# Four graph layers on one core: layer 1 aggregates before it projects, its logits are dot products on VectorE, small operations go to GpSimd

## The reference, cut to what matters

```python
h = relu(layernorm(x)); x = x + L0(h)      # x: 128 graphs, 128 nodes, 256 features
h = relu(layernorm(x)); x = x + L1(h)
h = relu(layernorm(x)); x = x + L2(h)
h = relu(layernorm(x)); x = x + L3(h)      # multi-head attention, 8 heads of 32

def L1(h):
    Wh = h @ W                                  # 256 x 256
    logits = leaky_relu((Wh @ a_src)[:, :, None] + (Wh @ a_dst)[:, None, :], 0.2)
    attn = softmax(where(adj == 0, -inf, logits), axis=-1)
    return nan_to_num(attn, nan=0.0) @ Wh
```

## Time and profile before

| | us |
|---|---|
| median of 3 runs | 1276.25 |
| lowest, highest | 1275.59, 1278.63 |
| the profiled execution, its own time | 1276.93 |
| its span in the profile | 1275.1 |

### The profile page before, as it was taken

How to read it: one execution, slowest core, us unless ns; L and a number is a source line. 1 busy time by engine, 2 the same in 40 slices (tenths; PEclk the granted TensorE clock), 3 DMA queues, 4 the chain that set the end, 5 groups by cost and what they waited for, 6 DMA issues and landing times. The chain is left out here.

```text
span 1275.1 us, 43341 instructions
## 1 busy us (share of the span) xinstructions
PE 1232.8 (97%) x12213; PEld 1134.8 (89%) x12213; DVE 1141.8 (90%) x5713; ACT 1058.2 (83%) x3911; POOL 944.5 (74%) x1338
## 2 busy tenths in 40 slices
PE   5799999999999999999999999999999999999997
PEld 4689999999999999999999998999999999999986
DVE  4689999989999999999999999999999999998874
ACT  2468898888888888888889888888889888888886
POOL 4568877877777877777787787777787777787663
PEclk9899999999999999999999999999999999999999
DMA  4011222222112122222112122222122122211001
GB/s 119 24 22 21 38 44 50 37 44 51 36 44 52 36 44 52 36 43 52 38 40 52 40 45 46 41 39 52 40 47 43 41 46 44 43 39 31 18 19 34
DMA packets 70586, 53.57 MB, mean 42 GB/s; under 512 B 20688, under 2 KB 70352, under 8 KB 70352
## 3 DMA queue, kind: packets, MB, share of 16 engines
q1 hardware_dynamic: 68144, 49.35, 19.2%
q10 hardware_dynamic: 2208, 1.45, 0.4%
HBM read 33.89 MB, written 16.89 MB: 40 GB/s over the span
## 5 line engine op out<-in xcount | busy, mean ns | idle before, releaser
L775 ACT ACTIVATE exps<-masked,nmax 128x128 f32<-128x128 f32 x1024 | 397.1, 394 | 0.0
L348 POOL TENSOR_TENSOR probs<-exps,rsum 128x512 f32<-128x512 f32 x256 | 266.7, 1042 | 162.6 <-DVE rsum L567 161.9
L319 POOL TENSOR_SCALAR y<-x,nm,rstd 128x256 f32<-128x256 f32 x512 | 282.8, 563 | 22.5 <-issue 21.0
L311 POOL TENSOR_TENSOR rstd<-veps,power 128x2 f32<-128x2 f32 x256 | 178.2, 696 | 114.4 <-DVE veps L472 109.3
L559 DVE CUSTOM_DVE_ANT_0 masked<-bank,mask 128x128 f32<-128x128 f32 x1024 | 232.0, 280 | 1.3 <-PE bank L986 0.8
L775 ACT ACTIVATION_READ_ACCUMULATOR exps<-masked,nmax 128x1 f32 x1024 | 198.4, 194 | 0.0
L876 PE MATMUL bank<-w_hi,ht_hi 128*128 128x512 f32 (+1 forms) x512 | 192.6, 376 | 4.5 <-DVE ht_lo L501 4.5
L456 DVE BATCH_NORM_STATS2 stats<-x 128x6 f32<-128x256 f32 x512 | 183.9, 411 | 0.2
L886 PE MATMUL bank<-ident,y 128*128 128x128 f32 x1024 | 159.0, 278 | 20.0 <-POOL y L319 19.3
L877 PE MATMUL bank<-w_lo,ht_hi 128*128 128x512 f32 (+1 forms) x512 | 175.4, 343 | 0.0
L878 PE MATMUL bank<-w_hi,ht_lo 128*128 128x512 f32 (+1 forms) x512 | 174.8, 341 | 0.0
(11 more groups left out here) (120 smaller groups left out, 3693.4 us busy)
## 6 DMA issues: line engine op xcount, KB each, us to landing
x<-in_x SPq DMA_DIRECT2D x64, 256.0 KB, 4.6
out<-x SPq DMA_DIRECT2D x64, 256.0 KB, 4.7
db<-rows SPq DMA_DIRECT2D x110, 128.0 KB, 4.1
rows<-dst SPq DMA_DIRECT2D x110, 1.0 KB, 3.0
probs<-in_w0t SPq DMA_DIRECT2D x1, 512.0 KB, 7.9
probs<-in_w1t ACTq DMA_DIRECT2D x1, 256.0 KB, 5.9
exps<-in_wot SPq DMA_DIRECT2D x1, 256.0 KB, 7.6
w_sb<-in_w ACTq DMA_DIRECT2D x1, 256.0 KB, 7.8
```

The source lines that it names most:

```text
L311: pool.tensor_tensor(rstd[i][:, b], veps[i][:, b], power[:], ALU.pow).then_inc(S[f"rstd{i}"], 1)
L319: last = pool.tensor_scalar(y[i][:, b, g], src[:, bx, g], nm[i][:, s, g:g + 1], rstd[i][:, s, g:g + 1], ALU.add, ALU.mult)
L348: pool.tensor_tensor(probs3[:, p % BUFFERS["probs3"], j], exps3[:, p % BUFFERS["exps3"], j], rsum3[:, s, j].unsqueeze(2).to_broadcast([P, ...
L775: last = act.activation(exps3[:, b, j, i], masked3[:, p % BUFFERS["masked3"], j, i], ACT.Exp, bias=nmax3[:, s, j, i:i + 1], scale=-1.0, ac ...
```

## The change

What it does, part by part:

- Layer 1 no longer transposes and projects `h` first. GpSimd forms `y1` = relu(x1 - mean) without the factor of the deviation (`centre1`). TensorE multiplies it with the transposed exponentials (`u_mm`, four fp32 matmuls of 128 columns), the result is split (`u_hi` on ScalarE, `u_lo` on VectorE) and then projected (`x2_mm`, the twelve fp32r matmuls). `h1t`, `h1t_hi`, `h1t_lo`, `wh0_mm`, `wh1_mm`, `wh0`, `wh1` and the old `x2_mm` go.
- The factor 1/deviation of a neighbour's row is put into the transposed exponentials: `at1` is two ScalarE copies of 128 columns with a scale per partition.
- The logits: VectorE takes four products with sum over 256 columns (`dots`), two with W a_dst, which stays in PSUM bank 7 (`w_dst`), and two with W a_src in SBUF (`w_src`). GpSimd multiplies them by the deviation's inverse into `ed1` (`dst1`, now for each pair), and SP writes `ed1` to DRAM itself.
- `veps` of all layers and the clearing of `rsum1` move from VectorE to GpSimd. `nm` goes: the mean is subtracted in `y` directly.
- All lags, the order of each engine's list and the banks are new; `y1` has three buffers.

```diff
@@ GpSimd
+            def shifted_variance(i, p):
+                b = p % SMALL
+                passed(pool, f"mv{i}", p)
+                passed(pool, f"rstd{i}", p, SMALL)
+                pool.tensor_scalar(veps[i][:, b], mv[i][:, b, :, 1], LN_EPS, None, ALU.add).then_inc(S[f"veps{i}"], 1)
+            def clear_empty_rows(p):
+                s = p % SMALL
+                passed(pool, "rsum1_any", p)
+                pool.tensor_tensor(rsum[1][:, s], rsum[1][:, s], has_any[:].to_broadcast([P, G]), ALU.mult).then_inc(S["rsum1"], 1)
+            def centre1(p):
+                b, s, bx = p % BUFFERS["y1"], p % SMALL, p % BUFFERS["x1"]
+                passed(pool, "mv1", p)
+                read_before(pool, "y1", p, "dots", "u_mm")
+                for g in range(G):
+                    last = pool.tensor_scalar(y[1][:, b, g], x1[:, bx, g], mv[1][:, s, g, 0:1], 0.0, ALU.subtract, ALU.max)
+                last.then_inc(S["y1"], 1)
+            def scale_dots(p):
+                b, s = p % BUFFERS["ed1"], p % SMALL
+                passed(pool, "dots", p)
+                passed(pool, "rstd1", p)
+                read_before(pool, "ed1", p, "z1")
+                pool.tensor_tensor(ed1[:, b], dots[:, s], rstd[1][:, s].unsqueeze(1).to_broadcast([P, 2, G]), ALU.mult).then_inc(S["dst1"], 1)
@@ VectorE
-                dve.tensor_scalar(veps[i][:, b], mv[i][:, b, :, 1], LN_EPS, None, ALU.add).then_inc(S[f"veps{i}"], 1)
-                dve.tensor_scalar(nm[i][:, b], mv[i][:, b, :, 0], -1.0, None, ALU.mult).then_inc(S[f"nm{i}"], 1)
+            def dot_products(p):
+                b, s = p % BUFFERS["y1"], p % SMALL
+                passed(dve, "y1", p)
+                dve.wait_ge(S["w1_split"], 1)
+                passed(dve, "dst1", p, SMALL)
+                passed(dve, "dots", p, 1)
+                for c, w in ((1, w_dst), (0, w_src[:])):
+                    for g in range(G):
+                        last = dve.tensor_tensor_reduce(weighted[:, c, g], w, y[1][:, b, g], scale=1.0, scalar=0.0, op0=ALU.mult, op1=ALU.add,
+                                                        accum_out=dots[:, s, c, g:g + 1])
+                last.then_inc(S["dots"], 1)
+            def low_u(p):
...
+                dve.tensor_tensor(ut_r[1][:, b].rearrange("p c g n -> p (c g n)"), bank_of("u")[:],
+                                  ut_r[0][:, b].rearrange("p c g n -> p (c g n)").bitcast(F32), ALU.subtract).then_inc(S["u_lo"], 1)
@@ ScalarE
-                act.activation(wh[:, b, g], bank_of(f"wh{g}")[:, 0:D + 2], ACT.Copy).then_inc(S[f"wh{g}"], 1)
+            def high_u(p):
...
+                act.activation(ut_r[0][:, b].rearrange("p c g n -> p (c g n)"), bank_of("u")[:], ACT.Copy).then_inc(S["u_hi"], 1)
+            def scale_exp_transposed1(p):
...
+                for g in range(G):
+                    last = act.activation(at[1][:, b, g], bank_of("at1")[:, g * P:(g + 1) * P], ACT.Copy, scale=rstd[1][:, s, g:g + 1])
@@ TensorE
+            def aggregate1(p):
+                b, ba = p % BUFFERS["y1"], p % BUFFERS["at1"]
+                passed(pe, "at1", p)
+                bank_free(pe, "u", p)
+                for c in range(DC):
+                    for g in range(G):
+                        last = pe.matmul(bank_of("u")[:, (c * G + g) * P:(c * G + g + 1) * P], y[1][:, b, g, c * P:(c + 1) * P], at[1][:, ba, g],
+                                         start=True, stop=True)
+            def project1(p):
+                b = p % BUFFERS["ut"]
+                passed(pe, "u_lo", p)
...
+                for g in range(G):
+                    for c in range(DC):
+                        last = split_matmul(bank_of("x2b")[:, g * D:(g + 1) * D], [u_[:, b, c, g] for u_ in ut_r], [w_[:, c, :] for w_ in w1_r],
+                                            c == 0, c == DC - 1)
```

More of the change, by code:

```diff
@@ L29 @@
 LAG = {
[11 rows of a table removed]
[11 rows of a table added]
 }
 BANKS = {
[L45 to L48, removed]
-    "v": (0, "v_mm", ('v',)),
[L50 to L75, removed]
+    "h0t": (5, "h0t", ('h0t_lo',)),
+    "pt1": (3, "pt1", ('p3t_1',)),
+    "qt": (4, "qt_mm", ('qt',)),
+    "x1b": (6, "s0", ('x1',)),
+    "kt": (0, "kt_mm", ('kt',)),
+    "d1": (3, "d1", ('z1',)),
+    "at2": (2, "e2t", ('at2',)),
+    "ot": (4, "ot_mm", ('ot_lo',)),
+    "sc0": (5, "scores", ('nmax3_0',)),
+    "sc1": (1, "scores", ('nmax3_1',)),
+    "sc2": (0, "scores", ('nmax3_2',)),
+    "sc3": (6, "scores", ('nmax3_3',)),
+    "h2t": (2, "h2t", ('ht2',)),
+    "x3b": (3, "x3_mm", ('x3',)),
+    "m0": (4, "m0", ('mj_lo0', 't0_0')),
+    "at1": (6, "e1t", ('at1',)),
+    "hh": (2, "hh_mm", ('hh',)),
+    "pt2": (3, "pt2", ('p3t_2',)),
+    "pt3": (5, "pt3", ('p3t_3',)),
+    "prep": (6, "products", ('w1_split',)),
+    "u": (6, "u_mm", ('u_lo',)),
+    "m1": (3, "m1", ('mj_lo1', 't0_1')),
+    "x4b": (2, "x4_mm", ('x4',)),
+    "v": (0, "v_mm", ('v',)),
+    "h3t": (4, "h3t", ('h3t_lo',)),
+    "x2b": (2, "x2_mm", ('x2',)),
+    "pt0": (6, "pt0", ('p3t_0',)),
+    "d2": (1, "d2", ('z2',)),
+    "prepa": (6, "adj_spread", ('adj_rows',)),
     "zz2": (7, "z2", ('nmax2',)),
@@ L110, in gnn_kernel @@
         warm = sb("warm", [P, G])
-        w1_sb = sb("w1_sb", [P, DC, D + 2])
+        w1_sb = sb("w1_sb", [P, DC, D])
         a1_sb = sb("a1_sb", [P, DC, 2])
@@ L272, in step @@
                     spread_row(2, t - LAG["row_in2"])
+                if due(t, "load") and t - LAG["load"] >= 2:
+                    load(t - LAG["load"])
             load(0)
@@ L357, in step @@
             def step(t):
+                if due(t, "rstd3"):
+                    inverse_deviation(3, t - LAG["rstd3"])
+                if due(t, "y3"):
+                    normalise(3, x3, t - LAG["y3"])
+                if due(t, "dst1"):
+                    scale_dots(t - LAG["dst1"])
+                if due(t, "veps0"):
+                    shifted_variance(0, t - LAG["veps0"])
+                if due(t, "rsum1"):
+                    clear_empty_rows(t - LAG["rsum1"])
+                if t == LAG["deg_b_made"]:
+                    prepare_deg_b()
@@ new lines, in step @@
+                if due(t, "veps2"):
+                    shifted_variance(2, t - LAG["veps2"])
+                if due(t, "rstd2"):
+                    inverse_deviation(2, t - LAG["rstd2"])
+                if due(t, "y2"):
+                    normalise(2, x2, t - LAG["y2"])
+                if due(t, "p3_2"):
+                    normalise_p3(2, t - LAG["p3_2"])
+                if due(t, "p3_0"):
+                    normalise_p3(0, t - LAG["p3_0"])
+                if due(t, "p3_3"):
+                    normalise_p3(3, t - LAG["p3_3"])
@@ L390, in step @@
[L390 to L401, removed]
+                if due(t, "veps3"):
+                    shifted_variance(3, t - LAG["veps3"])
@@ L585, in step @@
             def step(t):
+                if due(t, "stats0"):
+                    stats_of(0, x0, t - LAG["stats0"])
+                if due(t, "nmax3_3"):
+                    mask_scores(3, t - LAG["nmax3_3"])
+                if t == LAG["w1_split"]:
+                    split_w1()
+                if due(t, "x3"):
+                    sum_x3(t - LAG["x3"])
+                if due(t, "nmax3_0"):
+                    mask_scores(0, t - LAG["nmax3_0"])
+                if due(t, "stats3"):
+                    stats_of(3, x3, t - LAG["stats3"])
@@ new lines, in step @@
+                if due(t, "t0_0"):
+                    add_own(0, t - LAG["t0_0"])
+                if due(t, "rsum3_1"):
+                    inverse_sum3(1, t - LAG["rsum3_1"])
+                if due(t, "u_lo"):
+                    low_u(t - LAG["u_lo"])
+                if due(t, "x4"):
+                    sum_x4(t - LAG["x4"])
+                if due(t, "rsum1_any"):
+                    inverse_sum(1, "rsum1_any", "x2", t - LAG["rsum1_any"])
+                if due(t, "mj_lo1"):
+                    low_mj(1, t - LAG["mj_lo1"])
@@ L1073, in step @@
                     attend(2, hh, "hh", F1, t - LAG["x3_mm"])
-                if due(t, "wh1_mm"):
-                    project1(1, t - LAG["wh1_mm"])
+                if due(t, "m0"):
+                    project0(0, t - LAG["m0"])
+                if due(t, "e1t"):
+                    transpose_exp(1, t - LAG["e1t"])
                 if due(t, "hh_mm"):
                     project2(t - LAG["hh_mm"])
+                if due(t, "pt2"):
+                    transpose_p3(2, t - LAG["pt2"])
+                if due(t, "pt3"):
+                    transpose_p3(3, t - LAG["pt3"])
+                if t == LAG["products"]:
+                    multiply_weights()
+                if due(t, "u_mm"):
+                    aggregate1(t - LAG["u_mm"])
+                if due(t, "m1"):
+                    project0(1, t - LAG["m1"])
+                if due(t, "x4_mm"):
+                    project4(t - LAG["x4_mm"])
+                if due(t, "v_mm"):
```

(11 more changed lines are left out.)

367 lines of the change are left out of this document (146 added, 221 removed), and 22 rows, old and new, of the table LAG.

## The result

The changed kernel takes 1453.3 us (median of 4, 1452.7 to 1454.4), the kernel before beside it 1276.6: a ratio of 1.138 (95% interval 1.136 to 1.140). I had said 1256, with 1243 to 1286 around it and 71% for faster. The profiled execution of after has a span of 1451.6 us.

What follows compares the result with a forecast made beforehand. TensorE was taken to bound the kernel, busy for the whole 18.88 us step. 1276.93 - 25.6 (TensorE) + 7.0 (64 steps of 18.59 against 18.48) - 2 (ends) = 1256.3 us, given as 1256, range 1243 to 1286.

Steps and rivals of the forecast that it cites:

- L: Hold of VectorE's two `w_src` products behind GpSimd: between 0 and 1.13 us a step, taken as 0.4.
- TensorE, -0.40 us a step: Transposes `h1t` (-0.44) and old `x2_mm` (-0.86) go, `u_mm` (+0.90) comes: 18.48 us a step.
- VectorE: Small operations removed, 1.53 us, `dots` added, 1.38 us: 17.85 to 17.70 us a step, plus L.
- rival (c): Both `w_src` products held for a whole `y3` operation: step 19.3 us, 1304 us; chance 0.18 with milder forms above 1280.
- my sign for L = 0: In the profile after, the two `w_src` products would show a mean of 0.42 us.
- GpSimd: Four `veps`, `rsum1` and `dst1` as a product add 1.0 us a step on 14.9, bounds +0.9 and +3.4.
- the ring: Once-a-step loop from GpSimd's `rsum1` over `x3_tail` to VectorE's `stats3` and back: 18.2 us + L.
- the small operations at the price of the power: Sign of being wrong: GpSimd's small operations cost like the power, lengthening the ring by 0.5 for each in it.
- a bad place in a list: Sign of being wrong: an order placed by hand makes TensorE wait in each step for something else.

Runs made afterwards that it cites:

- e9: e8 with `y1` one place later in ScalarE's list, behind `p3t_2` instead of in front of it; 1249.1 us, 0.979 of the kernel before.
- e1: The changed kernel with ADD in place of SUBTRACT in the two GpSimd lines that form `y` (values differ); 1286.9 us, 1.007 of the kernel before.
- e3: The changed kernel with `nm` computed again on VectorE right behind `mv`, and all `y` by ADD; 1350.3 us, 1.057 of the kernel before.
- e7: The changed kernel with `nm` made on GpSimd, `y` by ADD and `veps1` moved in front of `y1`; 1365.4 us, 1.068 of the kernel before.
- e8: e7 with `y1` formed on ScalarE by Relu with bias `nm1`, in front of `p3t_2`; 1268.5 us, 0.991 of the kernel before.
- e5: e1 with SUBTRACT in `y2` alone; 1368.5 us.
- e6: e1 with SUBTRACT in `y3` alone; 1310.9 us.
- e4: GpSimd alone, sixteen of each of fourteen forms in a row, nothing of the four layers computed; ADD,MULT 557 ns, SUBTRACT,MULT 1223.

## Why the prediction was wrong

It was GpSimd's `y`, whose operation the change exchanged and whose price the sum left as it was. Term by term, with the row of the changed kernel on which L is read in front:

```profile
L537 DVE CUSTOM_DVE_ANT_0 weighted<-w_src,y 128x256 f32<-128x256 f32 x128 | 49.9, 427 | 0.0
```

- **TensorE, -0.40 us a step: right.** e9's step is 18.43 with PE busy throughout, against 18.88: -0.45.
- **VectorE: right in direction, and L was small.** `dots` cost the 1.38 us of the sum (e1: 614.68 to 616.06), and VectorE is busy 19 us less over the run, 0.3 a step, where the sum had 0.15 less, plus L. L, the hold of the two `w_src` products, was the unknown on which I put the range and the losing rival (c). The changed kernel has a mean of 427 ns for them, against 418 for the products with PSUM, though GpSimd's `y3` runs beside both (2.44 us from 613.50; the products start at 613.97 and 614.31). That was my sign for L = 0. It is not 0 in each order: in e3 and e7 the mean is 511 and 507, because one of the two is 0.2 us longer in every step. Rival (c) as priced did not happen. By the Trainium skill (SBUF - State Buffer, section Who interferes with whom), as I read it, the later one waits for the whole of the other. The traces do not show that here: a product loses nothing in a step of the changed kernel and 0.2 us in one of e3 or e7, and GpSimd's `y3` can be the one that is longer, 1.57 us for 1.10 in e1 and 1.52 in e7.
- **GpSimd: the step that failed.** I wrote that GpSimd "gets four `veps` and `rsum1`, and `dst1` becomes a product", +1.0 us. I left `y` at 563 ns in the sum of the ring and nowhere costed that its operation had changed. The edit is in the diff and looked like a renaming: it takes away `nm`, and the price of that was 5.1 us on GpSimd against 0.4 saved on VectorE (4 x 0.07 + 0.11). The 1.0 us that I did add was right: `veps`, `rsum1` and the product, less the old copy, come to 73 us, 1.1 a step. The row I needed was not in the trace of before: no tensor_scalar of that size with any other pair had run there. So it should have been bounded, by a row of another form. The nearest, a two-input operation of 128x256 at 686 ns, gives 0.12 us more each and would still have been too low.
- **The ring: right in form.** It was written as 18.2 us + L, with 12.5 on GpSimd; e1 has 13.63 there, and 12.5 without the 2 x 0.58 of a slow `y1`. With `y0` and `y2` at 1.23 and `y1` at 1.14 in place of 0.56 each it is 18.2 + 4 x 0.66 + 2 x 0.58 = 22.0; measured 21.73. With `y1` alone slow it is 19.4; e1 has 19.09. The forecast by that ring and the right price would have been 1276.9 + 64 x (22.0 - 18.88) = 1477 us.
- **Sum.** Of the 197 us between 1256 and 1453, 166 are SUBTRACT's (e1 against after). The other 31 lie between the forecast and e1, and e9, with `y1` off GpSimd, stands 38 under e1. By the ring that part is `y1`'s ADD,MAX, 2 x 0.58 us a step. This is argued and not shown: no run had `y1` on GpSimd at the fast pair's price, and e8 and e9 bring `nm` back and move `veps1` too.
- **The chances.** Only L was given a range up to a loss. None of the signs of being wrong that I named was this one: they were the small operations at the price of the power, and a bad place in a list. A range has to cover each operation whose form the trace of before does not show, not only the one that a rule calls dangerous.

## What to carry to other kernels

An operation is a form: engine, instruction, size, and also the pair of ALU operations. When an edit changes the pair, its price is unknown until a row shows it, and on GpSimd it moved by a factor of 2.2. Add up each ring that passes once a step through in-order queues: work in the ring costs nearly one for one (e5: 82 us for 87), work outside it less than half (e6: 24 for 62), whatever the busy shares say. And an operation moved to a less busy engine still takes its place in a queue: one place later was worth 16 to 19 us here (e8, e9).

## What the runs showed of the hardware that I had not expected

- GpSimd tensor_scalar, 128x256 fp32 (e4): ADD,MULT and MULT,ADD 557 ns; SUBTRACT,MULT and MULT,SUBTRACT 1223; ADD or SUBTRACT with MAX 1143; one operation alone, ADD or SUBTRACT, 925, more than the fast pair takes for two. Per column 0.83 and 3.3 ns. A strided scalar operand is without effect on ADD,MULT. tensor_tensor add and subtract are alike, 723.
- Two small GpSimd operations in a row (`nm` and `veps`, `veps` and `rstd` in e7) start 0.30 to 0.33 us apart, though the first is recorded with 0.22 to 0.25.
- A VectorE tensor_scalar of two columns in SBUF is held behind GpSimd for up to 1.0 us (e3: 1181 ns, against a median of 170).
- A VectorE product of two SBUF operands of 256 columns is held little or not at all beside GpSimd's `y3`: 0.42 us in the changed kernel, 0.61 to 0.63 for one of two in e7 and e3. GpSimd's operation with the fast pair is lengthened instead or as well (two in 1.57 us for 1.10 in e1); with the slow pair it is not (2.44 us beside the products, 2.43 for `y2` without them).
